# A decoder layer on one core: where the keys' weights stand in the load queues, keys loaded for two heads at a time, and the last row sums made by TensorE

## The reference

```python
x = x + ssm(layernorm(x))            # in-projection, conv of 4 taps, silu, then the recurrence
#   h = h * exp(A * dt_t) + (x_t * dt_t) * B_t ;  y_t = sum_n h[:, n] * C_t[n]     (1024 channels, 16 states)
x = x + attn(layernorm(x), ctx)      # 16 heads of 32; K = ctx @ Wk + bk, V = ctx @ Wv + bv
#   softmax(q k^T / sqrt(32)) v, then @ Wo + bo
x = x + moe(layernorm(x))            # router of two layers, 4 experts of 2048 hidden, top 2
```

## Time and profile before

| | us |
|---|---|
| three runs | 2546.5, 2555.25, 2561.81 |
| median | 2555.25 |
| the profiled execution, its own time | 2550.36 |
| its span in the profile | 2548.6 |
| mean granted clock of TensorE | 0.977 |

### The profile page before, as it was taken

The page is one execution under the profiler, slowest core; times in us unless marked ns, Lnnn a source line. Parts: engine busy times, 40 slices in busy tenths (PEclk is TensorE's granted clock), DMA queues, the critical chain, the costliest instruction groups (busy, mean ns, idle before and its releaser), DMA issues. The chain is left out here.

```text
span 2548.6 us, 39883 instructions
## 1 busy us (share of the span) xinstructions
PE 2407.9 (94%) x14548; PEld 2011.9 (79%) x14548; DVE 1475.2 (58%) x2051; ACT 1224.6 (48%) x2655; POOL 1377.7 (54%) x968
## 2 busy tenths in 40 slices
PE   6999899999999999979999999898999999999997
PEld 5867589999999996547667766664889998999996
DVE  7804599999999995446667766763422232212312
ACT  4335377778777763325444444442333332323332
POOL 2413378878887774355566656752580080006586
PEclk9999989999999999989999999889999999999999
DMA  4326876667765765465545554722431040002323
GB/s 113 133 66 209 247 218 204 183 183 215 205 197 170 208 203 138 122 152 138 121 122 137 138 133 110 182 59 83 146 132 48 33 150 29 33 16 96 107 77 109
DMA packets 233851, 341.97 MB, mean 134 GB/s; under 512 B 35199, under 2 KB 161799, under 8 KB 232661
## 3 DMA queue, kind: packets, MB, share of 16 engines
q1 hardware_dynamic: 214981, 286.22, 39.9%
q0 software_dynamic: 14624, 50.40, 6.3%
q10 hardware_dynamic: 4080, 3.18, 0.4%
HBM read 212.08 MB, written 127.65 MB: 133 GB/s over the span
## 5 line engine op out<-in xcount | busy, mean ns | idle before, releaser
L982 DVE TENSOR_TENSOR_SCAN s_h<-s_decay,s_ub 128x928 f32<-128x928 f32 x256 | 527.3, 2080 | 7.7 <-PE s_ub L1011 1.1
L1022 PE MATMUL s_yps<-s_hc,identity 128*128 128x224 f32 x2016 | 424.2, 353 | 0.7 <-POOL s_hc L846 0.4
L2239 DVE TENSOR_TENSOR e_hl<-e_ps,e_hh 128x256 fp32r<-128x256 f32 x256 | 107.8, 424 | 497.4 <-ACT e_ps L2313 497.4
L901 ACT ACTIVATE s_decay<-s_dt,s_A 128x224 f32<-128x224 f32 x1024 | 388.0, 472 | 0.0
L1370 DVE TENSOR_REDUCE t_nmax<-t_ps 112x1 fp32r<-112x752 f32 x256 | 240.3, 939 | 231.3 <-PE t_ps L1711 230.7
L1022 PEld LDWEIGHTS s_yps<-s_hc,identity 128*128 128x128 f32 x2016 | 362.5, 190 | 2.7 <-POOL s_hc L846 2.2
L2312 ACT ACTIVATE e_hh<-e_ps,e_b 128x256 fp32r<-128x256 f32 x256 | 121.8, 476 | 500.0 <-PE e_ps L2349 499.8
L1326 POOL TENSOR_TENSOR t_part<-t_pT 125x672 f32<-125x672 f32 x128 | 206.8, 1615 | 257.3 <-ACT t_pT L1616 254.4
L1616 ACT ACTIVATE t_pT<-t_ps 125x448 f32<-125x448 f32 x384 | 180.9, 545 | 252.7 <-PE t_ps L1737 252.4
L846 POOL TENSOR_TENSOR s_hc<-s_h,carry 128x896 f32<-128x896 f32 x128 | 247.9, 1946 | 74.8 <-DVE s_h L982 49.4
L846 POOL TENSOR_TENSOR s_hc<-s_h,s_Cc 128x896 f32<-128x896 f32 x128 | 247.9, 1947 | 68.6 <-DVE s_h L982 49.9
(11 more groups left out here) (263 smaller groups left out, 5125.3 us busy)
## 6 DMA issues: line engine op xcount, KB each, us to landing
s_ut<-ut_d SPq DMA_DIRECT2D x192, 128.0 KB, 3.3
carry<-in_L_ffn_We POOLq DMA_DIRECT2D x24, 1024.0 KB, 5.8
t_k<-kh_d SPq DMA_DIRECT2D x64, 375.0 KB, 6.5
xs_d<-s_zero SPq DMA_DIRECT2D x30, 512.0 KB, 4.0
ut_d<-a_x SPq DMA_DIRECT2D x31, 448.0 KB, 5.4
kh_d<-s_kh SPq DMA_DIRECT2D x32, 375.0 KB, 3.0
kl_d<-s_kl SPq DMA_DIRECT2D x32, 375.0 KB, 3.4
v_d<-s_v SPq DMA_DIRECT2D x48, 250.0 KB
```

The source lines that it names most:

```text
L901: ins = nc.scalar.activation(decay[:, u % 2, :, n, 2:SLOT], dts[:, u % 2].rearrange("p (s t) -> p s t", s=NSEG), ACT.Exp, scale=A[:, u % C ...
L982: nc.vector.tensor_tensor_scan(h[:, k].rearrange("p n t -> p (n t)"), decay[:, u % 2, k].rearrange("p n t -> p (n t)"), ub[:, s % 2, AT:AT ...
L1022: ins = nc.tensor.matmul(yps[:, u % 2, 0:L], ident[:], hc[:, u % 2, :, n], start=(n == 0), stop=(n == NS - 1))
```

## The change

It has three parts. In the recurrence, `Wk`, the context of batch 0, `bk`, `Wv` and `D` leave ScalarE's queue and are issued by SP, behind `C` 0 and ahead of `ut` 1. In the attention, the keys of a group are loaded in two halves of two heads, each with its own semaphore; the first half is issued at slot `4J - 4` and the second at `4J - 2`, each when the two heads whose place it takes have had their turned scores. And the row sums of the last group are made from the exponentials by TensorE, behind the last `values`, and GpSimd no longer adds those four heads.

```diff
             def load_ctx(b):
-                sp.wait_ge(ctx_split, b)
+                if b >= 1:
+                    sp.wait_ge(ctx_split, b)
...
             load_c(0)
+            sp.dma_start(wk_raw, Wk.rearrange("(k p) n -> p k n", p=P)).then_inc(consts, 16)
+            load_ctx(0)
+            sp.dma_start(bkc[:], bk).then_inc(consts, 16)
+            sp.dma_start(wv_raw, Wv.rearrange("(k p) n -> p k n", p=P)).then_inc(consts, 16)
+            sp.dma_start(Dv[:], D).then_inc(consts, 16)
             load_ut(1)
...
-            act.dma_start(wk_raw, Wk.rearrange("(k p) n -> p k n", p=P)).then_inc(consts, 16)
-            act.dma_start(cxT, ctxT_in[0].rearrange("(k p) t -> p k t", p=P)).then_inc(ctx_loaded, 16)
-            act.dma_start(bkc[:], bk).then_inc(consts, 16)
-            act.dma_start(wv_raw, Wv.rearrange("(k p) n -> p k n", p=P)).then_inc(consts, 16)
-            act.dma_start(Dv[:], D).then_inc(consts, 16)
...
-            def load_keys(J):
+            def load_keys(J, half):
                 if J >= 2:
-                    sp.wait_ge(st_mm, 3 * 4 * (J - 1))
+                    sp.wait_ge(st_mm, 3 * (4 * (J - 2) + 2 * half + 2))
                 for i, src in PARTS:
-                    sp.dma_start(k3[i * DK:(i + 1) * DK, J % 2].bitcast(F32),
-                                 src[J // KC, J % KC].rearrange("(r p) t -> p r t", p=DK)).then_inc(k_loaded[J % 2], 16)
+                    sp.dma_start(k3[i * DK:(i + 1) * DK, J % 2, 2 * half:2 * half + 2].bitcast(F32),
+                                 src[J // KC, J % KC, 2 * half * DK:2 * (half + 1) * DK].rearrange("(r p) t -> p r t", p=DK)
+                                 ).then_inc(k_loaded[2 * (J % 2) + half], 16)
...
-                if sl % 4 == 2 and among((s + 2) // 4, B * KC) and s >= 6:
-                    load_keys((s + 2) // 4)
+                if sl % 2 == 0 and among((s + 4) // 4, B * KC) and s >= 4:
+                    load_keys((s + 4) // 4, sl % 4 // 2)
...
-                if among(s - LAG, STEPS):
+                if among(s - LAG, STEPS - 4):
                     row_sum(s - LAG)
...
-                if u == 0 and h % 4 == 0:
-                    pe.wait_ge(k_loaded[J % 2], 48 * (J // 2 + 1))
+                if u == 0 and h % 2 == 0:
+                    pe.wait_ge(k_loaded[2 * (J % 2) + h % 4 // 2], 48 * (J // 2 + 1))
...
+            def last_row_sums():
+                J = B * KC - 1
+                for r in range(4):
+                    for i in range(NC):
+                        ins = nc.tensor.matmul(ps[DK * r:DK * r + DK, PV_BANK, L:2 * L], ones[:], pT[:, (4 * J + r) % PT, i],
+                                               start=(i == 0), stop=(i == NC - 1), tile_position=(0, DK * r))
+                ins.then_inc(sums_mm, 1)
...
                     values((s - PV_LAG) // 4)
+                    if (s - PV_LAG) // 4 == B * KC - 1:
+                        last_row_sums()
-                if (s - SUM_LAG) % 4 == 0 and among((s - SUM_LAG) // 4, B * KC):
+                if (s - SUM_LAG) % 4 == 0 and among((s - SUM_LAG) // 4, B * KC - 1):
                     row_sums((s - SUM_LAG) // 4)
```

More of the change, by code:

```diff
@@ L1155, in attention @@
         q_first = [sem(f"q_first{j}") for j in range(KC)]
-        k_loaded, q_stored = ([sem(f"{n}{i}") for i in range(2)] for n in ("k_loaded", "q_stored"))
+        k_loaded, q_stored = ([sem(f"{n}{i}") for i in range(count)] for n, count in (("k_loaded", 4), ("q_stored", 2)))
         v_loaded = [sem(f"v_loaded{j}") for j in range(KC)]
@@ L1257, in _ @@
                 sp.dma_start(dst, src).then_inc(w_loaded, 16)
-            load_keys(0)
-            load_keys(1)
+            for J in range(2):
+                for half in range(2):
+                    load_keys(J, half)
             sp.dma_start(bor[:], bo.partition_broadcast(P)).then_inc(bo_loaded, 16)
```

## The result

The changed kernel takes 2571.01 us (median of 19 runs, 2559.57 to 2578.11), the kernel before 2559.24 us beside it (19 runs, 2546.5 to 2565.73). The ratio is 1.0045 with an interval from 1.0032 to 1.0059: about 11.6 us slower. The prediction's bound for "hardly to be told from none" was 0.5%, 12.8 us; the interval reaches just past it. Forecast were 2561.0, or +5.9 us on before. The sign was right, and the sum was half of what came.

A forecast was written before the change was run, and what follows sets the result against it. VectorE and TensorE were taken to bound the recurrence, TensorE the attention. Parts A +3.0, B -3.9 and C +6.8 gave +5.9 us on the profiled 2550.36, 2556.3, or 2561 on the median's footing; range 2548 to 2573.

The forecast's parts named there:

- The stages: Whole kernel: recurrence, attention and experts follow so tightly that each part costs in the total what it costs at its place.
- The weights were put at 325.5: Recurrence start: D, last of the weights' transfers, lands at 325.5, upper bound 327, making VectorE's low part 3.0 us late.
- The step on the first scan: Recurrence start: bt lands 2.6 us earlier without the weights beside it, so the first scan starts at 319.0 instead of 321.60.
- the 0.8 us for each iteration: Attention, slot 8 of 7 iterations: query stores delayed behind the keys' first half cost 0.8 us each, +5.6 (0 to 15).
- the first rival: Attention, slot 8 of seven iterations: stores held up 2.2 us each, +15.4 instead of +5.6, total 2571; chance 0.12.
- The room of 1.19 on VectorE: Attention, slot 8: VectorE's low part started 1.19 us behind ScalarE's end, so of 1.9 us late some 0.7 pass on.
- a batch of the attention over 2 us longer: Attention: the prediction is wrong if a batch, 85.55 us from 1117.83 to 1203.38 before, becomes over 2 us longer.
- The order does not matter: Last row sums: column group order is of no account, part C -0.5 us, total -1.4, 2554; chance 0.10.
- the weights land in time: Recurrence start: weights land before the first scan is over, part A -2.6 us, total +0.3, 2555.5; chance 0.06.
- Not felt at all: Attention, slot 8: the query stores do not feel the keys' half, total +0.3 us, 2555.5; chance 0.17.
- The wait stays: Attention, head 0 of batch 1: TensorE waits as long for keys, part B +4.6 us, total +14.4, 2569.5; chance 0.09.
- Held up for long: Attention, slot 8: stores held up 2.2 us an iteration, total +15.7, 2571, deciding from 1.8 us; chance 0.12.

The follow-up runs named there:

- after: The changed kernel with all three parts of the diff, against the kernel before: 2571.01 us, ratio 1.0045.
- b_only: Only the keys by halves, as in the diff, on the kernel before: +0.5 us by the ratio.
- b_quarter: Keys by halves alone on the kernel before, but in iterations 1 to 6 slot 8 loads only head 0's keys, head 1's following behind the stores: five batches 429.6 us.
- best: Kernel before plus halved keys (slot 8's behind the stores in iterations 1 to 6) and TensorE sums, heads inside, no idle products before end_project: 0.9967.
- c_only: Only the last row sums on TensorE, head in the outer loop as in the diff, on the kernel before: +4.4 us by the ratio.

## Why the prediction was right, and where it was not

The forecast was near for the sum and not for its parts. Part A cost more than forecast, part B was forecast as a gain and was none, and part C cost less. The errors partly cancel, so that the sum stayed within 0.5% (11.6 of 12.8 us) is in part luck.

**The stages.** That each part costs at its place what it costs in the total was not contradicted: the three parts' times add up to the whole, within intervals of 10 us each.

**Part A, +3.0 forecast; +3.9 in the profile of after, +6.1 by the time of the part alone.** The mechanism was the one forecast: ScalarE waits for D, VectorE's low part starts late. Two terms were off. The weights were put at 325.5, which is 19.9 us behind the first idle product; four profiles show 19.8 to 23.0, two of them above the upper bound of 327. In after it was 20.3, and the low part of Wk came 3.3 us late for the 3.0 forecast. And the prediction took what follows that low part as unchanged, while the low part of Wv grew from 2.69 to 3.20 us. That this instruction depends on GpSimd could have been read ahead of time in the timeline of before, where it took 2.69 us and its twin 1.20. The step on the first scan failed too: bt came early as forecast, the scan 0.7 instead of 2.6 earlier, since the idle products stood ahead of fill 0. As the prediction had put the second scan behind the weights "whatever was won", that had no price. With C 0 behind them in the queue the weights landed 3.9 to 7.2 us earlier. That agrees with the rule on the order of a queue that the prediction took from the Trainium skill (DMA: Bandwidth & Descriptors, Queues, rings and completion order).

What held the low part stands in the Trainium skill (SBUF — State Buffer, SBUF: two separate sides): a VectorE instruction with two inputs in SBUF and a GpSimd instruction that reads SBUF share a pair of ports, which the one that starts first holds to its end. The eleven low parts that ended 1.08 to 1.17 us behind GpSimd's instruction agree with it, and so does the 2.83 above.

**Part B, -3.9 forecast; +0.5 by the time of the part alone, with an interval from -4.9 to +5.6, and +3 to +5 by the profiles (6.9 to 7.7 us won from batch 0 to 1, 10.5 to 11.9 of waits in the six iterations behind it).** The gain came near the 8.5 forecast (7.5 for the wait and 1.0 for the clock), but not by those terms: in after 5.5 us of it are head 0's earlier start and 2.1 the full clock behind it. The wait itself vanished in part because TensorE came later. The term that failed is the 0.8 us for each iteration. TensorE stood still for 11.2 us in the seven iterations of after and for 12.5 in those of b_only, 1.6 and 1.8 each, where 5.6 in all were forecast and 15.4 by the first rival. Where it went wrong: the second store was put 2.3 us late, between 1.3 and 4.0. It was issued 1.4 later, and took 1.8 longer to land (2.7 in b_only). Block 2 was 3.15 us late on average instead of 1.9. The room of 1.19 on VectorE was read rightly, as b_quarter shows, so that almost the whole error of the first number went through to TensorE: 3.15 less 1.19 is 1.96, and the waits of these six iterations are 1.75 on average. The prediction took the middle of a range in which only the lower part was free of cost.

One of the prediction's signs of being wrong, a batch of the attention over 2 us longer, did show in the stretch that it names, and decides nothing. From head 0 of batch 1 to head 0 of batch 2 it is 90.0 us in after and 88.7 in b_only, where it was 85.6 before; but the seven kernels without part B, before among them, need 85.4 to 92.2.

**Part C, +6.8 forecast; +4.1 in the profile of after, +4.4 by the time.** The mechanism was right and the size of one term off: neighbours on the same 32 columns don't run beside each other as those on four groups do, but one costs 0.147 to 0.155 us and not the 0.21 of products on all 128 columns, so the sums take 7.1 to 7.5 us instead of 9.5. Why it is 0.147 was not looked for; it also means that the four groups of the values' loop don't run wholly beside each other, as the prediction had worked out from 12 x 0.207. What follows the sums took 4.0, forecast 3.8. The page of the Trainium skill that was named there (TensorEngine Tiling (Array Packing), Performance Considerations) allows four times the speed for four groups; the orders stand at 0.147 against 0.051, 2.9 times.

**The rivals.** "The order does not matter" and "the weights land in time" fell. "Not felt at all" fell, but is true of a delay of up to 1.1 us. "The wait stays" fell; 3.8 us of it were left with the halves and without the early place. "Held up for long", priced at 2.2 us an iteration against the forecast's 0.8, was the nearer of the two: 1.6 and 1.8 came, and it was to decide from 1.8.

## What to carry to other kernels

When a transfer is moved ahead of another in a queue, price both: the issues ahead of it and the bytes ahead of it, and set the sum against the room of every engine behind; the cost is zero up to that room and full beyond it, so the middle of a range is a poor guess. Products that use part of TensorE's columns belong in an order in which neighbours lie on different columns. When an instruction moves in time, look at what its twin takes where another engine works beside it: a row that is longer than its twin points at a neighbour to look for. And a wait that is gone from a timeline may be gone because the waiter came late: compare when each of the two arrived.

## What the runs showed of the hardware beyond what was expected

- Products of 32 columns (125 rows, 224 columns moving): 0.051 us an instruction when four neighbours lie on four groups (best), and 0.147 when they lie on one (after), both at granted clock 1.00; 0.155 in c_only at 0.94; a full product of 128 columns takes 0.21.
- A subtraction on VectorE with two inputs of 128x1024 takes 1.20 us. When an instruction of GpSimd is under way it ends 1.08 to 1.17 beyond the other's end, 1.20 to 4.13 us in all. GpSimd's instruction that starts behind VectorE's is held in turn, 2.8 to 2.9 us for 1.94. The scans of 2.09 us were not touched by GpSimd's products beside them.
- A store of 112 KB lands in 3.6 to 4.2 us beside the values' load (iterations 1 to 6 of before), and in 5.6 to 6.6 with 0.56 MB of keys ahead of it in the queue; with half of those, in 3.6 to 4.0 again.
- The same five batches took 424.2 to 437.2 us in kernels that don't differ there. TensorE's idle time in them was 22.9 to 30.6 us and half clock took 1.7 to 6.8; the rest was 399.1 to 400.0. Why TensorE stands still longer in one batch than in another stays open.
